# Two Mamba layers on one core: where TensorE's other work stands between the two halves of a scan step's sum

## The reference, cut to what matters

```python
def step(h, inp):
    d_t, B_t, x_t, C_t = inp
    dA = jnp.exp(d_t[..., None] * A)
    h = dA * h + (d_t * x_t)[..., None] * B_t[:, None, :]
    y = jnp.einsum('bdn,bn->bd', h, C_t)
    return (h, y)
```

## Time and profile before

| what | value |
|---|---|
| median of three runs | 2034.77 us (2033.21 to 2038.48) |
| the profiled execution, its own time | 2036.81 us |
| its span, first to last instruction | 2034.9 us |
| mean granted TensorE clock | 0.974 of full speed |
| GpSimd (POOL) busy | 1937.6 us, 853 instructions |
| TensorE (PE) busy | 1833.8 us, 4972 matmul instructions |
| VectorE (DVE) busy | 1787.9 us, 1063 instructions |
| ScalarE (ACT) busy | 1149.4 us, 1179 instructions |

### The profile page before, as it was taken

The page is one execution under the profiler, slowest core; times in us unless marked ns, Lnnn a source line. Parts: engine busy times, 40 slices in busy tenths (PEclk is TensorE's granted clock), DMA queues, the critical chain, the costliest instruction groups (busy, mean ns, idle before and its releaser), DMA issues. The chain is left out here.

```text
span 2034.9 us, 16945 instructions
## 1 busy us (share of the span) xinstructions
PE 1833.8 (90%) x4972; PEld 686.9 (34%) x4972; DVE 1787.9 (88%) x1063; ACT 1149.4 (56%) x1179; POOL 1937.6 (95%) x853
## 2 busy tenths in 40 slices
PE   7899889898899899899899889989989988987778
PEld 3333333333343233233333333323323323332332
DVE  3889897868989988987898997998798999699998
ACT  4657565657657446654756745744584574554332
POOL 1999999999999999999999999999999999999997
PEclk9899999999999899999999999999999999999899
DMA  5558558665766877676776787776666677667676
GB/s 148 206 203 210 208 206 208 207 225 180 191 240 217 202 231 255 174 233 212 210 199 219 214 222 233 228 201 243 212 172 207 224 208 215 233 219 207 210 224 153
DMA packets 127623, 427.86 MB, mean 210 GB/s; under 512 B 18524, under 2 KB 23020, under 8 KB 127532
## 3 DMA queue, kind: packets, MB, share of 16 engines
q1 hardware_dynamic: 127532, 426.79, 68.9%
HBM read 416.29 MB, written 6.29 MB: 208 GB/s over the span
## 5 line engine op out<-in xcount | busy, mean ns | idle before, releaser
L987 POOL TENSOR_TENSOR ring<-ring,c_ring 128x1024 f32<-128x1024 f32 x575 | 1346.2, 2369 | 38.3 <-DVE ring L932 33.0
L560 PE MATMUL y_ps<-ring,wp 128*128 128x512 f32 x2304 | 1148.3, 616 | 10.9 <-DVE yv_rows L912 4.5
L932 DVE TENSOR_TENSOR_SCAN ring<-a_ring,b_ps 128x1024 f32<-128x1024 f32 x368 | 841.1, 2286 | 31.6 <-issue 0.5
L560 PEld LDWEIGHTS y_ps<-ring,wp 128*128 128x128 f32 x2304 | 428.1, 194 | 522.5 <-issue 439.8
L932 DVE TENSOR_TENSOR_SCAN ring<-b_ps,b_ring 128x1024 f32<-128x1024 f32 x208 | 471.1, 2274 | 75.1 <-ACT b_ps L732 26.5
L980 POOL TENSOR_TENSOR b_ring<-u_ab,b_ring 128x1024 f32<-128x1024 f32 x161 | 381.9, 2372 | 8.9 <-DMA b_ring<-bc_rows 8.9
L541 PE MATMUL b_ps<-b_in,sel 96*64 96x512 bf16 (+1 forms) x1020 | 230.3, 402 | 143.5 <-DVE ring L932 141.8
L732 ACT ACTIVATE a_ring<-delta_ab,wp 128x1024 f32<-128x1024 f32 x223 | 251.9, 1140 | 158.4 <-DVE ring L932 155.2
L897 DVE TENSOR_TENSOR b_ps<-u_ab,b_ps 128x1024 f32<-128x1024 f32 x223 | 270.3, 1212 | 64.6 <-PE b_ps L541 56.5
L732 ACT ACTIVATE b_ps<-delta_ab,wp 128x1024 f32<-128x1024 f32 x161 | 179.8, 1117 | 208.3 <-DVE ring L932 207.8
L725 ACT ACT_TABLE_LOAD x186 | 238.6, 1283 | 52.7 <-DVE ring L932 49.8
(11 more groups left out here) (97 smaller groups left out, 849.5 us busy)
## 6 DMA issues: line engine op xcount, KB each, us to landing
c_ring<-bc_rows SPq DMA_DIRECT2D x384, 512.0 KB, 4.7
c_ring<-bc_rows SPq DMA_DIRECT2D x384, 256.0 KB, 4.4
b_ring<-bc_rows SPq DMA_DIRECT2D x161, 512.0 KB, 5.3
b_ring<-bc_rows SPq DMA_DIRECT2D x94, 256.0 KB, 5.4
out<-io SPq DMA_DIRECT2D x16, 192.0 KB, 5.0
bc_rows<-bc_out SPq DMA_DIRECT2D x22, 128.0 KB, 5.3
io<-x SPq DMA_DIRECT2D x6, 384.0 KB, 6.2
b_in<-parts SPq DMA_DIRECT2D x24, 96.0 KB, 2.3
```

The lines of the kernel that those rows point to most:

```text
L560: nc.tensor.matmul(half(y_ps[:, :], j), ident, half(ring[:, g % RING, :], j), start=(n == 0 and kind == FWD), stop=(n == NS - 1)).then_inc ...
L932: nc.vector.tensor_tensor_scan(out=h, data0=a, data1=b, initial=0.0, op0=ALU.mult, op1=ALU.add).then_inc(h_ready, 1)
L987: nc.gpsimd.tensor_tensor(r, r, c, ALU.mult).then_inc(g_ready, 1)
```

## The change: jobs ahead of both halves

One tuple is written in another order. In each of TensorE's slots the slot's jobs come right behind `ahead`, and then both halves of the sum of step g - 4 follow one another. Instructions, operands, buffers, waits and the other engines' orders stay as they are. In slots without a job TensorE's stream is the same as before.

```diff
-PE_ORDER = ("ahead", "sum_0", "jobs", "sum_1")
+PE_ORDER = ("ahead", "jobs", "sum_0", "sum_1")
 ACT_ORDER = ("ahead_a2", "ahead_a", "jobs")
 SP_ORDER = ("ahead_b", "ahead_c", "jobs")
 POOL_ORDER = ("ahead_b", "product", "jobs")
```

## The result

The changed kernel takes 2048.5 us (median of four runs, 2047.7 to 2051.2) against 2034.7 us: a ratio of 1.0064, 95% interval 1.0052 to 1.0077, so 10.6 to 15.7 us more. The profiled execution has 2047.72 us of its own and a span of 2045.8 us, 10.9 us more than the span before. A second execution with a profile, taken later, has 2044.2 us and a span of 2042.4, less than any of the four. So the traces show 10.9 us (8.8 us between the second executions) of the 13.8 us by which the medians differ; the profiled execution of before was itself 2.0 us above its median.

A forecast was written before the change was run, and what follows sets the result against it. TensorE sets the pace in slots full of jobs, with GpSimd living on its lead; in thin slots TensorE waits for the scan. Terms 3.8 + 2.6 + 0.9 + 0.9 + 0.9 = 9.1 us gave 2043.9 us, range 2031 to 2052.

The forecast's parts named there:

- The mechanism: In about 27 slots the first half no longer covers a job's wait for its bank; at most 23 us.
- BWD 0, 1, 2, slot 4: The job waits for its bank with no half ahead, so each slot ends 1.27 us later; 3.8 us in all.
- FWD 0: In slots 8, 22 and 31 a half no longer covers the job's wait; 0.86 us each, 2.6 in all.
- The first half later: The take of a finished tile waits for the half that now runs behind the jobs; put at nothing.
- Slot 8's own term: In slot 8 of FWD 0 the job's wait loses its cover; 0.86 us, reaching a GpSimd wait.
- Rival C: Late takes in eleven of the slots 3, 19 and 35 cost 18.6 us, giving 2053; chance 0.06.
- FWD 3, slot 4: A job's wait of 1.32 us loses its cover; 0.9 us, as GpSimd waits at 1743.81.
- FWD 1, slot 31: A job's wait of 1.22 us loses the half that covered it; 0.9 us.
- ROWS 0: In slots 10 and 11 only one half is lost over two waits; 0.9 us more GpSimd wait at 132.25.
- Jobs earlier by a half: ScalarE gets job results 0.86 to 1.72 us sooner, but VectorE's next step follows TensorE's next slot; nothing.
- rival B: Faster: earlier ScalarE decays shrink VectorE's and GpSimd's waits, 7.5 us less, 2027.3; countered by full TensorE; chance 0.10.
- Rival A: No change: GpSimd alone is the bound and its lead absorbs small pieces; 0 to 6 us, say 2036; chance 0.34.

The follow-up runs named there:

- bwd_slot4: Kernel before, with the jobs ahead of both halves only in slot 4 of BWD 0, 1 and 2; 2039.65 us against 2035.54, ratio 1.0023.
- named_ten: Changed kernel, with the order of before in the ten slots that the prediction's sum names; 2037.5 us, ratio 1.0015.
- covered: Changed kernel, with the order of before in 34 slots: 33 where a job came to wait, and slot 3 of FWD 0; 2031.6 us, ratio 0.9986.
- not_fwd0_slot3: Changed kernel, with the order of before in slot 3 of FWD 0 alone; 2044.6 us, ratio 1.0045.
- not_fwd0: Changed kernel, with the order of before in all 48 slots of FWD 0; 2042.9 us, ratio to before 1.0039.
- fwd0_slot3: Kernel before, with the jobs first in slot 3 of FWD 0 alone; 2038.3 us in one execution.
- rows1_only: Kernel before, with the jobs first in slots 28 to 41 of ROWS 1 alone; 2033.6 us in one execution.
- rows0_three: Kernel before, with the jobs first in slots 10, 11 and 36 of ROWS 0 alone; 2035.8 us in one execution.
- jobs_last: Kernel before, with the jobs behind both halves of the sum in every slot; 2057.0 us, ratio 1.0106.

## Why the prediction was right, point by point

- **The mechanism** (a first half that no longer runs during a wait for a bank) is right, shown by bwd_slot4, named_ten and covered. The count of about 27 such slots was low; the two traces show 33 in which a job came to wait. GpSimd's waits for VectorE came to 42.2 us, as forecast; that it fits so well is partly luck, since the terms did not each hold. The time grew by 13.8 us, where the sum had 9.1.
- **BWD 0, 1, 2, slot 4**, 3.8 us: right. 1.4 us in each item, 4.2 in all.
- **FWD 0**, 2.6 us: mis-sized, 4.4 to 6.2 measured. The step that failed is "The first half later (...) I put it at nothing". From the item's start to step 11, GpSimd loses 0.4 us against before in not_fwd0_slot3 and 2.4 in the second execution of the changed kernel: slot 3's late take is worth 2.0 us where slot 8 has the new order too (0.8 by itself), and it acts through ScalarE on the bank of slot 8 (a wait of 2.38 us against 1.12). Slot 8's own term is right (in not_fwd0_slot3 the second half is 0.86 us later behind it than ahead of it), but its path is not: it reaches GpSimd at the DMA wait behind step 10, where the prediction looked at step 20. In the first execution the low clock behind slot 8 makes the 2.4 us 3.6. Slot 22, counted at 0.86, costs 0.5 (at step 25 GpSimd waits 2.37 us for 1.86; with the old order 1.88). The rest, 1.6 us in the second execution and 2.2 in the first, comes at steps 34 and 35 behind a low clock from 496.5 and 510.5 us. In not_fwd0 the same 1.6 us stand there, and half of them are hidden, since its clock rose 2 us earlier at slot 3; that is its 0.8 us left. Both executions of the changed kernel have this low clock and neither of before has it; whether the change brings it is not shown. Rival C's mechanism is thus real in one of its eleven places; at step 36 of ROWS 1, where the take waits 4.29 us, GpSimd waits 0.35, and the time is far from its 18.6 us. Of slot 31, counted at 0.86 us, no run shows a share: GpSimd's wait at step 35 is 1.8 us where the clock fell just before, with the old order too (not_fwd0, fwd0_slot3), and 0.2 to 0.4 where it did not.
- **FWD 3, slot 4**, 0.9 us: the place is right, the end is not. GpSimd's wait at step 10 goes from 0.28 to 1.14 us, exactly 0.86 more; its wait at step 40, 0.83 us before, is then gone, and the item is no longer.
- **FWD 1, slot 31**, 0.9 us: not shown. 173.4 us is 0.7 and 1.8 more than the item has with the old order and a full clock (172.7 in bwd_slot4, 171.6 in rows1_only), and 1.0 less than in before; the clock falls within the item in before and in the changed kernel, so the share of slot 31 can't be told.
- **ROWS 0**, 0.9 us for slots 10 and 11: right, 0.8 in rows0_three. Slot 36 was not in the sum, and it costs 1.3 us on TensorE; of that some 0.5 reached GpSimd at step 11 of ROWS 1 in rows0_three. What it costs in the changed kernel is open, since the clock falls near that slot there (169.2 to 172.6 us).
- **"Jobs earlier by a half (...) nothing"**: wrong as a view of VectorE, which waits 19.9 us less for decays, and jobs_last shows the price of the reverse. It was nearly right for the time, since in the full stretches the waits for TensorE took that place, as rival B's counter-argument said.
- **What wasn't thought of** is two gains: 1.5 us of TensorE's time in ROWS 1, and GpSimd's wait at step 6 of ROWS 0 (1.61 us before, 1.51 in its second execution), which is gone in both executions of the changed kernel and in covered (though it is 0.70 us in fwd0_slot3, with the old order there, so not all of it need be the order's). In the changed kernel the waits at steps 20, 21 and 24 (0.60, 0.42 and 3.12 us, before only 2.60 at step 24) take it back.
- **Rival A** fell: GpSimd is 95% busy before and after, and the time still rose. The rule of the Trainium skill that the prediction weighed (Perfetto Trace Analysis, Identifying the Most-Contended Engine) would have said 0 us; TensorE's weight loads have 34% in both profiles, and the stretches in which it is full decided.

## What to carry to other kernels

Where two engines hand a few buffers to and fro, put work that is ready ahead of an instruction that may have to wait, slot by slot: look for the slots where the wait is, and leave the order alone elsewhere (at most 34 of 253 slots decided here, and a mixed order beat all three pure ones). Price such a move in the stretch in which the engine has no gap, and add what follows through the other engines' own order; the wait that is lost first (slot 8) may have been set up several slots earlier (slot 3). An order between two extremes may be near the best since it splits two waits, so look at both totals before it is moved. And before two runs are subtracted, see where TensorE's clock was low in each: two runs whose clock rose 2 us apart gave the take waits that differ by 1.0 us for the same order.

## What the runs showed of the hardware

- A float32 half of the sum takes 0.86 us between matmuls with 128 columns of weights and 1.06 us between groups with 64. The Trainium skill, page TensorEngine Tiling (Array Packing), section Key Properties, says that a change of the tiling mode drains TensorE; the 0.2 us would agree with it, though no run here shows that these forms are such modes.
- The place at which TensorE's granted clock falls to 0.50 can differ between two executions of one kernel. Behind one and the same gap of 2.4 us, with TensorE busy for 1.61 and 1.62 of the 4 us up to its end, it fell in one execution of the changed kernel and stayed at 1.00 in the other. Another fall, near 998.5 us, stood in both executions of before and was gone where only earlier work had been moved.
- A stretch of low clock cost 1.6 to 1.7 us where TensorE was the pace (step 35 of FWD 0 in fwd0_slot3 and not_fwd0, slot 4 of BWD 1 in bwd_slot4).
